# A recommendation tower on one core: the perceptron over pairs of tiles in place of single tiles

## The chip, the core and the metric

The kernel runs on one core of a Trainium2 chip. The metric is the device time of one execution in microseconds (us). Each engine runs its own instruction stream: TensorE (PE; its weight loads are listed apart as PEld), VectorE (DVE), ScalarE (ACT), GpSimd (POOL) and SyncE (SP). They meet only through semaphores and DMA.

## The reference

For 2048 samples, 32 embedding rows of 16 numbers are looked up, all 496 dot products of two of them are taken, and a perceptron of three layers (512, 256, 1) runs over these and 16 dense features. All is in float32.

```
e = jnp.stack([tbl_0[ids[:, 0]], ..., tbl_31[ids[:, 31]]], axis=1)     # [2048, 32, 16]
z = jnp.sum(e[:, row, :] * e[:, col, :], axis=2)                       # 496 pairs row < col of the 32 fields
h = jnp.concatenate([z, dense_ctx], axis=1)                            # [2048, 512]
h = jnp.maximum(h @ W_top1 + b_top1, 0.0)                              # 512 x 512
h = jnp.maximum(h @ W_top2 + b_top2, 0.0)                              # 512 x 256
y = h @ W_top3                                                         # 256 x 1
```

## The kernel before, in words

The samples are worked in 16 tiles of 128 (the partitions). Of the 32 fields, 17 have small tables (1000 or 1250 rows); these are kept on chip and looked up by TensorE with one-hot matrices in six "rounds" (`look_up`, L640 and L645), from which VectorE picks the row with a maximum (`pick`, L470). The other 15 fields are gathered from HBM by GpSimd, one indirect DMA for each field and tile (L367), in three groups of 7, 5 and 3 fields, written straight into `emb`, which has room for all tiles.

What sets the order on GpSimd: after every fifth gather (`RUN`) it waits until that gather has landed (L373), except in the last tile, 15, where the 15 gathers follow each other without this. From tile 2 on it also waits, ahead of each group, until VectorE has multiplied the same group two tiles earlier (L358).

VectorE multiplies the pairs (L480, L489, L498, L508) into `prod`, a group as soon as its fields have landed, and itself sums the last 112 pairs (`sum_pairs`, L517). TensorE sums and turns the other 384, in three chunks of 128: `sum_chunk` (L663) is 16 accumulating transposes, `turn` (L670) one for the chunk that VectorE summed. The result stands in PSUM with features on the partitions; ScalarE copies it to `zT` (`copy_z`, L882).

The perceptron of the program before takes one tile at a time, 128 samples as columns: `layer1(t, place, n)` for n = 0 to 3 (L683, 4 matmuls each of 128x128 weights by 128 columns, float32), `relu1` on ScalarE (L888), `layer2(t)` (L692, 8 matmuls), `relu2` (L893), `layer3(t)` (L699, 2 matmuls with a single weight column), `copy_y` (L899). A float32 matmul of this kind leaves two records in the trace (a transpose and a bf16 matmul leave one), so that one `layer1` chunk is 8 records and `layer2` is 16.

All engines step through "windows", one for each tile t, in an order written out by hand: in window t TensorE finishes chunk 2 and the turn of tile t-1, runs layers 2 and 3 of tile t-2, layer 1 of tile t-1, the look-ups of tile t+1 and the first round or two of t+2, and chunks 0 and 1 of tile t. Windows 0 and 1 are straight code, 2 to 13 a loop over pairs of windows, 14 straight again. The end (from L763 on TensorE, L968 on ScalarE) treats tile 15 with orders of its own: `add_chunks` (L780) runs layer 1 chunk by chunk as its inputs come, then layer 2 (L803) and layer 3 (L811). On ScalarE `relu1(14, 2)` and `relu1(14, 3)` stand ahead of `copy_end` (L981) and of the copies of the second group of tile 15 (`copy_group`, L875 and L877), on which VectorE's last products wait. The result is stored in two DMAs, the second of tile 15 alone (L335).

## Time and profile before

| | |
|---|---|
| median of 3 runs | 390.46 us (387.18, 390.46, 392.57) |
| span of the profiled execution | 386.4 us |
| time of the profiled execution | not listed apart; the nearest run is 387.18, 0.8 us above the span |
| TensorE, weight loads | 299.7 us busy (78%), 267.2 us (69%) |
| VectorE | 248.2 us (64%) |
| GpSimd | 228.5 us (59%) |
| ScalarE | 145.3 us (38%) |
| mean granted TensorE clock | 0.925 |

The span is that from the first to the last instruction on the core; what a run takes beyond it lies around it. A share of busy time says how much work an engine has, not whether anything waits for it. A gather counts as GpSimd's work only while the instruction runs, not while its data are under way.

### The profile page before, as it was taken

What the parts mean: (1) busy time and instruction counts of PE and PEld (TensorE: products, weight loads), DVE (VectorE), ACT (ScalarE), POOL (GpSimd) and SP (SyncE); (2) the same over time, 40 slices, a digit from 0 to 9 for tenths busy, and PEclk for the clock granted to TensorE, in tenths of its full rate; (3) what the DMA queues carried; (4) which work ended last, traced back from release to release, by engine and by line L of the source; (5) the groups of instructions that cost most, each with busy time, mean ns of one, the idle gap of its engine ahead of it and who ended that gap; (6) DMA issues with size and microseconds to landing.
All of it is one profiled execution on the core that took longest, in us unless ns stands there. A gap on an engine that the chain in (4) does not pass through costs nothing.

```text
span 386.4 us, 7087 instructions
## 1 busy us (share of the span) xinstructions
PE 299.7 (78%) x2572; PEld 267.2 (69%) x2572; DVE 248.2 (64%) x326; ACT 145.3 (38%) x311; POOL 228.5 (59%) x250
## 2 busy tenths in 40 slices
PE   1767799886987967988676887877699786978477
PEld 1356689785887856877665886766598675867366
DVE  7699758675666666493756739464683955557541
ACT  3883543443162525244332424424243441113012
POOL 6456655566566656656665666566556656666700
PEclk9889779998999999989999998999969899899859
DMA  6670020202020202102020110202002000000000
GB/s 141 205 242 7 8 64 8 64 8 65 7 63 5 65 5 49 21 6 63 6 64 5 40 29 6 64 6 65 6 9 60 5 7 5 8 6 8 6 2 3
DMA packets 19036, 14.51 MB, mean 38 GB/s; under 512 B 9727, under 2 KB 16461, under 8 KB 19022
## 3 DMA queue, kind: packets, MB, share of 16 engines
q1 hardware_dynamic: 10284, 11.69, 9.5%
q0 software_dynamic: 7680, 1.98, 5.9%
q10 hardware_dynamic: 1058, 0.66, 0.6%
q8 instruction: 8, 0.13, 0.1%
q14 instruction: 6, 0.05, 0.0%
HBM read 14.24 MB, written 0.08 MB: 37 GB/s over the span
## 4 chain that ended last, share of the span: by engine, by line
issue 33%; POOL 28%; DMA 15%; PE 9%; DVE 6%; another core or an unknown queue 4%; ACT 3%; DVEq 1%; ACTq 0%; POOLq 0%
POOL emb L367 28%; DMA emb<-tbl,idx 15%; DVE emb L470 2%; PE bank L683 2%; DVE prod L489 2%; PE bank L663 2%; PE bank L692 1%; PE bank L645 1%; PE bank L780 1%; DVE prod L498 1%; ACT h1T L888 1%; ACT distance L844 1%; ACT onehot L854 1%; DMA idx<-ids 1%
## 5 line engine op out<-in xcount | busy, mean ns | idle before, releaser
L367 POOL DMA_INDIRECT emb<-tbl,idx x240 | 227.3, 947 | 138.4 <-DMA emb<-tbl,idx 73.4
L489 DVE TENSOR_TENSOR prod<-emb,bank 128x1904 f32<-128x1904 f32 (+5 forms) x51 | 94.5, 1854 | 88.3 <-DMA emb<-tbl,idx 88.3
L663 PE MATMUL bank<-ident,prod 128*128 128x128 f32 x768 | 102.8, 287 | 14.0 <-issue 8.6
L663 PEld LDWEIGHTS bank<-ident,prod 128*128 128x128 f32 x768 | 94.4, 197 | 15.9 <-issue 9.9
L683 PE MATMUL bank<-zT,w_sb 128*128 128x128 f32 x480 | 70.6, 295 | 13.6 <-ACT zT L882 12.9
L645 PE MATMUL bank<-parts,onehot 125*128 125x160 bf16 (+1 forms) x816 | 77.0, 244 | 1.4 <-issue 1.3
L683 PEld LDWEIGHTS bank<-zT,w_sb 128*128 128x128 f32 x480 | 63.6, 207 | 16.7 <-issue 14.9
L645 PEld LDWEIGHTS bank<-parts,onehot 125*128 125x128 bf16 x816 | 66.2, 106 | 12.3 <-issue 4.6
L470 DVE TENSOR_REDUCE emb<-bank 128x480 f32 (+5 forms) x96 | 52.7, 584 | 17.2 <-PE bank L645 8.8
L640 PE MATMUL bank<-far_ten,named_ten 100*128 100x480 bf16 (+1 forms) x64 | 24.8, 388 | 33.1 <-issue 24.5
L888 ACT ACTIVATE h1T<-bank,b_sb 128x128 f32<-128x128 f32 x60 | 21.5, 363 | 65.9 <-PE bank L683 26.5
L875 ACT COPY bank<-emb 128x112 f32 (+3 forms) x32 | 7.8, 243 | 100.0 <-issue 81.2
L480 DVE TENSOR_TENSOR prod<-bank,emb 128x2176 f32<-128x2176 f32 x16 | 38.7, 2419 | 7.2 <-ACT bank L868 6.4
L517 DVE TENSOR_REDUCE z_last<-prod 128x22 f32<-128x352 f32 (+3 forms) x32 | 34.8, 1087 | 2.2
L854 ACT ACTIVATE onehot<-distance,one 125x1152 bf16<-125x1152 bf16 (+1 forms) x30 | 35.8, 1195 | 0.0
L844 ACT ACTIVATE distance<-gids,minus_row 125x1152 bf16<-125x1152 f16 (+1 forms) x30 | 34.4, 1193 | 0.2
L640 PEld LDWEIGHTS bank<-far_ten,named_ten 100*128 (+1 forms) x64 | 6.9, 108 | 39.1 <-issue 32.0
L692 PE MATMUL bank<-h1T,w_sb 128*128 128x128 f32 x240 | 31.9, 288 | 1.0 <-issue 0.8
L692 PEld LDWEIGHTS bank<-h1T,w_sb 128*128 128x128 f32 x240 | 29.7, 201 | 1.9 <-issue 1.5
L498 DVE TENSOR_TENSOR prod<-bank,emb 128x336 f32<-128x336 f32 (+1 forms) x32 | 13.2, 411 | 8.7 <-ACT emb L877 7.7
L882 ACT COPY zT<-bank 128x512 f32<-128x512 f32 x15 | 8.8, 585 | 25.7 <-remote 22.8
L640 PE MATMUL bank<-far_eight,named_eight 70*128 70x512 bf16 (+1 forms) x32 | 11.3, 354 | 8.2 <-DVE emb L470 5.1
(71 smaller groups left out, 126.5 us busy)
## 6 DMA issues: line engine op xcount, KB each, us to landing
gids<-small_ids_f SPq DMA_DIRECT2D x16, 544.0 KB
emb<-tbl,idx POOLq DMA_INDIRECT x240
w_sb<-w SPq DMA_DIRECT2D x1, 1024.0 KB
w_sb<-w SPq DMA_DIRECT2D x1, 512.0 KB
tab<-tbl SPq DMA_DIRECT2D x7, 56.0 KB
tab<-tbl SPq DMA_DIRECT2D x5, 70.0 KB
tab<-tbl ACTq DMA_DIRECT2D x5, 70.0 KB
z_last<-dense SPq DMA_DIRECT2D x16, 8.0 KB
```

Of the source, the lines that this page charges most:

```text
L367: nc.gpsimd.indirect_dma_start(emb[:, t, at:at + D], None, tables[f], bass.IndirectOffsetOnAxis(ap=idx[:, t, f:f + 1], axis=0)).then_inc(d ...
L470: nc.vector.tensor_reduce(emb_at(t, SMALL_PLACE + first, n).rearrange("p a x -> p (a x)"), bank[:, from_bank, 0:width_of(r)].rearrange("p ...
L480: nc.vector.tensor_tensor(prod[:, 0:PAIR_AT[1] * D].rearrange("p (k x) -> p k x", k=SHIFTS), strided(bank[:, E_BANK, 0:S * D], [[0, SHIFTS ...
L489: return nc.vector.tensor_tensor(prod[:, at * D:(at + n * a) * D].rearrange("p (j i d) -> p j i d", j=n, d=D), strided(emb_at(t, PLACES[g] ...
L517: nc.vector.tensor_reduce(z_last[:, place, first - SUM_AT:end - SUM_AT], prod[:, first * D:end * D].rearrange("p (a d) -> p a d", d=D), AX ...
L640: nc.tensor.matmul(bank[:, to_bank, 0:n * w], named[0:rows, bass.ts(t, P)], far[0:rows, field * w:(field + n) * w], start=True, stop=False)
L645: mm = nc.tensor.matmul(look, onehot[:, place, i, :], parts[:, k, CAND_AT[i] * D:CAND_AT[i + 1] * D], start=False, stop=(i == first + n - ...
L663: mm = nc.tensor.matmul(bank[:, Z_BANK + place, c * P:(c + 1) * P], v[:, d, :], ident[:], start=(d == 0), stop=(d == D - 1), is_transpose= ...
L683: mm = nc.tensor.matmul(bank[:, H1_BANK + n % 2, 0:P], w1_sb[:, c, n * P:(n + 1) * P], zT[:, place, c, :], start=(c == 0), stop=(c == CHUN ...
L692: mm = nc.tensor.matmul(bank[:, H2_BANK, m * P:(m + 1) * P], w2_sb[:, c, m * P:(m + 1) * P], h1T[:, c, :], start=(c == 0), stop=(c == H1 / ...
L844: nc.scalar.activation(distance[:, first * P:(first + n) * P].rearrange("p (f j n) -> p f j n", f=n, n=SUB), gids[0:ROWS, place, :].rearra ...
L854: nc.scalar.activation(onehot[:, place, first:first + n, :].rearrange("p f b -> p (f b)"), distance[:, first * P:(first + n) * P], ACT.Rel ...
```

## The change

Layers 1 to 3 now take "units". Units 0 to 6 are the tile pairs (0,1) to (12,13), with 256 columns a matmul; tiles 14 and 15 are units of one tile each, as before with 128 columns. `zT`, `h1T` and `h2T` hold two tiles side by side; the two results of a pair go to columns 256 to 511 of PSUM bank 4. In an even window t (2, 4, ...) TensorE runs chunks 0, 1 and 2 of layer 1 of the pair (t-2, t-1); in the odd window behind it chunk 3, both chunks of layer 2 and layer 3. Windows 0 and 1 hold no perceptron work any more. The weights, look-ups, sums, gathers, products and the treatment of tile 15 are the same. On GpSimd nothing is changed, and on VectorE only the semaphore counts at the end.

```diff
         z_last = sb("z_last", [P, 2, (CHUNKS - TURN_SUMS) * P])
-        zT = sb("zT", [P, 2, CHUNKS, P])
-        h1T = sb("h1T", [P, H1 // P, P])
-        h2T = sb("h2T", [P, H2 // P, P])
+        zT = sb("zT", [P, CHUNKS, 2, P])
+        h1T = sb("h1T", [P, H1 // P, 2 * P])
+        h2T = sb("h2T", [P, H2 // P, 2 * P])
         y = sb("y", [1, B])
         w1_sb = sb("w1_sb", [P, CHUNKS, H1])
         w2_sb = sb("w2_sb", [P, H1 // P, H2])
...
+
+        PAIR_Y_BANK = 4
 
         END_H1_BANK, END_H2_BANK = (3, 4, 6, 7), (5, 0)
...
+
+        PAIRS = TILES // 2 - 1
+        LAST_UNIT = PAIRS + 1
+
         def steps_done(t, step):
...
                 pe.wait_ge(dense_loaded[place], loads * 16)
                 turn(place, 3)
 
-            def layer1(t, place, n):
+            def z_of(c, half):
+
+                return zT[:, c, :, :].rearrange("p h b -> p (h b)") if half is None else zT[:, c, half, :]
+
+            def layer1(unit, n, tiles, half=None):
+                cols = P if half is not None else 2 * P
                 if n == 0:
-                    pe.wait_ge(z_copied, t + 1)
-                pe.wait_ge(h1_done, 4 * t + n + 1)
+                    pe.wait_ge(z_copied, tiles)
+                pe.wait_ge(h1_done, 4 * unit + n + 1)
+                if n == 1:
+                    pe.wait_ge(y_copied, unit + 1)
                 for c in range(CHUNKS):
-                    mm = nc.tensor.matmul(bank[:, H1_BANK + n % 2, 0:P], w1_sb[:, c, n * P:(n + 1) * P],
-                                          zT[:, place, c, :], start=(c == 0), stop=(c == CHUNKS - 1))
+                    mm = nc.tensor.matmul(bank[:, H1_BANK + n % 2, 0:cols], w1_sb[:, c, n * P:(n + 1) * P],
+                                          z_of(c, half), start=(c == 0), stop=(c == CHUNKS - 1))
                 mm.then_inc(h1_ready, 1)
 
-            def layer2(t):
-                pe.wait_ge(y_copied, t + 1)
-                pe.wait_ge(h1_done, 4 * t + 4 + 2)
-                for m in range(H2 // P):
-                    for c in range(H1 // P):
-                        mm = nc.tensor.matmul(bank[:, H2_BANK, m * P:(m + 1) * P], w2_sb[:, c, m * P:(m + 1) * P],
-                                              h1T[:, c, :], start=(c == 0), stop=(c == H1 // P - 1))
+            def layer2(unit, m, cols=2 * P, together=False):
+                if m == 0:
+                    pe.wait_ge(y_copied, unit + 1)
+                    pe.wait_ge(h1_done, 4 * unit + 4 + 2)
+                elif not together:
+                    pe.wait_ge(h2_done, 2 * unit + 1)
+                for c in range(H1 // P):
+                    mm = nc.tensor.matmul(bank[:, H2_BANK, m * cols:(m + 1) * cols], w2_sb[:, c, m * P:(m + 1) * P],
+                                          h1T[:, c, 0:cols], start=(c == 0), stop=(c == H1 // P - 1))
                 mm.then_inc(h2_ready, 1)
 
-            def layer3(t):
-                pe.wait_ge(h2_done, 2 * t + 2)
+            def layer3(unit, y_bank=PAIR_Y_BANK, cols=2 * P):
+                pe.wait_ge(h2_done, 2 * unit + 2)
                 for c in range(H2 // P):
-                    mm = nc.tensor.matmul(bank[0:1, H2_BANK, Y_COL:Y_COL + P], w3_sb[:, c:c + 1],
-                                          h2T[:, c, :], start=(c == 0), stop=(c == H2 // P - 1))
+                    mm = nc.tensor.matmul(bank[0:1, y_bank, Y_COL:Y_COL + cols], w3_sb[:, c:c + 1],
+                                          h2T[:, c, 0:cols], start=(c == 0), stop=(c == H2 // P - 1))
                 mm.then_inc(y_ready, 1)
 
-            def window(t, place, loads, before=2, look=True, ahead=True):
-
-                if before > 0:
-                    sum_chunk(t - 1, 1 - place, 2, GROUP1_STEP)
-                    turn_sums(t - 1, 1 - place, loads)
-                if before > 1:
-                    layer2(t - 2)
-                if before > 0:
-                    layer1(t - 1, 1 - place, 0)
-                if before > 1:
-                    layer3(t - 2)
-                if look:
-                    look_up_rounds(t + 1, 1 - place, (2, 3))
-                sum_chunk(t, place, 0, SMALL_STEP)
-                if before > 0:
-                    layer1(t - 1, 1 - place, 1)
-                else:
-
-                    pe.wait_ge(masks_made, 2 * n_masks)
-                    turn_masks(1)
-                if look:
-                    look_up_rounds(t + 1, 1 - place, (4, 5))
-                if before == 0:
-                    pe.wait_ge(named_made, 3)
-                    turn_masks(2)
-                sum_chunk(t, place, 1, CIRCLE0_STEP)
-                if before > 0:
-                    layer1(t - 1, 1 - place, 2)
-                else:
-                    pe.wait_ge(named_made, 6)
-                    turn_masks(3)
+            def first_window():
+
+                look_up_rounds(1, 1, (2, 3))
+                sum_chunk(0, 0, 0, SMALL_STEP)
+                pe.wait_ge(masks_made, 2 * n_masks)
+                turn_masks(1)
+                look_up_rounds(1, 1, (4, 5))
+                pe.wait_ge(named_made, 3)
+                turn_masks(2)
+                sum_chunk(0, 0, 1, CIRCLE0_STEP)
+                pe.wait_ge(named_made, 6)
+                turn_masks(3)
+                look_up_rounds(2, 0, (0,))
+                look_up_rounds(2, 0, (1,))
+
+            def even_window(t, unit, ahead=True):
+
+                sum_chunk(t - 1, 1, 2, GROUP1_STEP)
+                turn_sums(t - 1, 1, unit + 1)
+                look_up_rounds(t + 1, 1, (2, 3))
+                layer1(unit, 0, 2 * unit + 2)
+                sum_chunk(t, 0, 0, SMALL_STEP)
+                layer1(unit, 1, 2 * unit + 2)
+                look_up_rounds(t + 1, 1, (4, 5))
+                sum_chunk(t, 0, 1, CIRCLE0_STEP)
+                layer1(unit, 2, 2 * unit + 2)
                 if ahead:
-                    look_up_rounds(t + 2, place, (0,))
-                if before > 0:
-                    layer1(t - 1, 1 - place, 3)
-                if ahead:
-                    look_up_rounds(t + 2, place, (1,))
+                    look_up_rounds(t + 2, 0, (0,))
+                    look_up_rounds(t + 2, 0, (1,))
+
+            def odd_window(t, unit, loads, after_pair=True):
+
+                if after_pair:
+                    layer1(unit, 3, 2 * unit + 2)
+                sum_chunk(t - 1, 0, 2, GROUP1_STEP)
+                turn_sums(t - 1, 0, loads)
+                look_up_rounds(t + 1, 0, (2, 3))
+                sum_chunk(t, 1, 0, SMALL_STEP)
+                if after_pair:
+                    layer2(unit, 0)
+                look_up_rounds(t + 1, 0, (4, 5))
+                sum_chunk(t, 1, 1, CIRCLE0_STEP)
+                if after_pair:
+                    layer2(unit, 1)
+                look_up_rounds(t + 2, 1, (0,))
+                if after_pair:
+                    layer3(unit)
+                look_up_rounds(t + 2, 1, (1,))
 
             pe.wait_ge(masks_made, n_masks)
             pe.wait_ge(ident_bf_ready, 1)
...
+            odd_window(1, 0, 1, after_pair=False)
             with pe.Fori(0, (TILES - 4) // 2) as j:
-                window(2 * j + 2, 0, j + 1)
-                window(2 * j + 3, 1, j + 2)
-            window(TILES - 2, 0, TILES // 2 - 1, ahead=False)
+                even_window(2 * j + 2, j)
+                odd_window(2 * j + 3, j, j + 2)
+            even_window(TILES - 2, PAIRS - 1, ahead=False)
+            layer1(PAIRS - 1, 3, TILES - 2)
 
             t = LAST_TILE
             sum_chunk(t - 1, 0, 2, GROUP1_STEP)
-            layer2(t - 2)
-            layer3(t - 2)
+            layer2(PAIRS - 1, 0)
+            layer2(PAIRS - 1, 1, together=True)
+            layer3(PAIRS - 1)
             turn_sums(t - 1, 0, TILES // 2)
-            layer1(t - 1, 0, 0)
-            layer1(t - 1, 0, 1)
+            layer1(PAIRS, 0, t, half=0)
+            layer1(PAIRS, 1, t, half=0)
             sum_chunk(t, 1, 0, SMALL_STEP)
-            layer1(t - 1, 0, 2)
-            layer1(t - 1, 0, 3)
+            layer1(PAIRS, 2, t, half=0)
+            layer1(PAIRS, 3, t, half=0)
             sum_chunk(t, 1, 1, CIRCLE0_STEP)
...
 
-            def relu1(t, n):
-                act.wait_ge(h1_ready, 4 * t + n + 1)
-                nc.scalar.activation(h1T[:, n, :], bank[:, H1_BANK + n % 2, 0:P], ACT.Relu,
+            def relu1(unit, n, cols=2 * P):
+                act.wait_ge(h1_ready, 4 * unit + n + 1)
+                nc.scalar.activation(h1T[:, n, 0:cols], bank[:, H1_BANK + n % 2, 0:cols], ACT.Relu,
                                      bias=b1_sb[:, n:n + 1]).then_inc(h1_done, 1)
 
-            def relu2(t, m):
-                act.wait_ge(h2_ready, t + 1)
-                nc.scalar.activation(h2T[:, m, :], bank[:, H2_BANK, m * P:(m + 1) * P], ACT.Relu,
+            def relu2(unit, m, cols=2 * P, together=False):
+                act.wait_ge(h2_ready, 2 * unit + (2 if together else m + 1))
+                nc.scalar.activation(h2T[:, m, 0:cols], bank[:, H2_BANK, m * cols:(m + 1) * cols], ACT.Relu,
                                      bias=b2_sb[:, m:m + 1]).then_inc(h2_done, 1)
 
-            def copy_y(t):
-                act.wait_ge(y_ready, t + 1)
+            def copy_pair_y(unit):
+                act.wait_ge(y_ready, unit + 1)
                 act.nop(nofuse=True)
...
+                copy_group(0, 1, GROUP1_STEP)
...
-                    onehots(t + 2, place, 1)
-                if before > 0:
-                    relu1(t - 1, 1)
-                else:
-                    copy_named(2)
+                    onehots(t + 2, 0, 1)
+                relu1(unit, 1)
                 copy_group(t, 1, GROUP1_STEP)
-                if before == 0:
-                    copy_named(3)
-                if look:
-                    wrap(t + 1)
-                if before > 0:
-                    relu1(t - 1, 2)
-                    relu1(t - 1, 3)
-                if before > 1:
-                    copy_y(t - 2)
-                if look:
-                    copy_small(t + 1)
+                wrap(t + 1)
+                relu1(unit, 2)
+                if not ahead:
+                    relu1(unit, 3)
+                copy_small(t + 1)
+
+            def odd_window(t, unit, loads, after_pair=True):
+
+                distances(t + 2, 1, 0, loads)
+                distances(t + 2, 1, 1, loads)
+                if after_pair:
+                    relu1(unit, 3)
+                copy_z(t - 1, 0)
+                onehots(t + 2, 1, 0)
+                copy_group(t, 0, GROUP0_STEP)
+                onehots(t + 2, 1, 1)
+                if after_pair:
+                    relu2(unit, 0)
+                copy_group(t, 1, GROUP1_STEP)
+                wrap(t + 1)
+                if after_pair:
+                    relu2(unit, 1)
+                    copy_pair_y(unit)
+                copy_small(t + 1)
 
             act.dma_start(idx[:, 0, :], ids[:, 0, :]).then_inc(first_ids_loaded, 16)
```

In the loop on TensorE one turn handles two tiles. Of before, from the first window of a turn to the third chunk of layer 1 (L683 is layer 1, L692 layer 2, L699 layer 3, L663 a chunk of sums, L640 and L645 the look-ups):

```order
70 L683 MATMUL bank<-zT,w_sb 128x128 x4
72 L699 MATMUL bank<-h2T,w_sb 1x128 x2
76 L645 MATMUL bank<-parts,onehot 128x160 x6
79 L645 MATMUL bank<-parts,onehot 128x160 x6
81 L663 MATMUL bank<-ident,prod 128x128 x16
83 L683 MATMUL bank<-zT,w_sb 128x128 x4
```

Of the changed program, the same stretch (L696 is layer 1):

```order
65 L651 MATMUL bank<-parts,onehot 128x160 x6
68 L651 MATMUL bank<-parts,onehot 128x160 x6
71 L696 MATMUL bank<-zT,w_sb 128x256 x4
73 L669 MATMUL bank<-ident,prod 128x128 x16
75 L696 MATMUL bank<-zT,w_sb 128x256 x4
```

The instructions are as many for a pair as they were for a tile, with twice the columns, and the first chunk of layer 1 now stands behind the look-ups.

TensorE after window 14, before (from the last layer 1 of tile 13 to the second half of layer 1 of tile 14):

```order
162 L683 MATMUL bank<-zT,w_sb 128x128 x8
163 L663 MATMUL bank<-ident,prod 128x128 x16
164 L692 MATMUL bank<-h1T,w_sb 128x128 x8
165 L699 MATMUL bank<-h2T,w_sb 1x128 x2
166 L670 MATMUL bank<-ident,z_last 128x128
167 L683 MATMUL bank<-zT,w_sb 128x128 x8
168 L663 MATMUL bank<-ident,prod 128x128 x16
169 L683 MATMUL bank<-zT,w_sb 128x128 x8
170 L663 MATMUL bank<-ident,prod 128x128 x16
```

and now:

```order
145 L696 MATMUL bank<-zT,w_sb 128x256 x8
146 L669 MATMUL bank<-ident,prod 128x128 x16
147 L707 MATMUL bank<-h1T,w_sb 128x256 x8
148 L714 MATMUL bank<-h2T,w_sb 1x256 x2
149 L676 MATMUL bank<-ident,z_last 128x128
150 L696 MATMUL bank<-zT,w_sb 128x128 x8
151 L669 MATMUL bank<-ident,prod 128x128 x16
152 L696 MATMUL bank<-zT,w_sb 128x128 x8
153 L669 MATMUL bank<-ident,prod 128x128 x16
```

The order is the same; the three steps that belonged to tile 13 now belong to the pair (12,13) and have 256 columns.

ScalarE in the same stretch, before and, behind the dots, now:

```order
157 L882 COPY zT<-bank 128x512
158 L888 ACTIVATE h1T<-bank,b_sb 128x128 x2
159 L875 COPY bank<-emb 128x112
160 L877 COPY emb<-emb 128x48
161 L888 ACTIVATE h1T<-bank,b_sb 128x128 x2
162 L981 COPY zT<-bank 128x256
...
147 L911 COPY zT<-bank 128x4x128
148 L917 ACTIVATE h1T<-bank,b_sb 128x128 x2
149 L904 COPY bank<-emb 128x112
150 L906 COPY emb<-emb 128x48
151 L917 ACTIVATE h1T<-bank,b_sb 128x128 x2
152 L1032 COPY zT<-bank 128x2x128
```

Nothing moved here: the copies of the first group of tile 15 still stand behind the first two rectifications of tile 14, and `copy_end` behind the other two.

## Rows read from the trace of the kernel before

**Rows 1.** The page, part 1: busy us, share of the span and instructions of each engine.

```profile
PE 299.7 (78%) x2572; PEld 267.2 (69%) x2572; DVE 248.2 (64%) x326; ACT 145.3 (38%) x311; POOL 228.5 (59%) x250
```

**Rows 2.** Waits of the whole span: engine line, waited for, us in total, times, longest.

```profile
DVE prod L489 <- DMA emb<-tbl,idx: 88.3, 25, 5.3
POOL emb L367 <- DMA emb<-tbl,idx: 73.4, 42, 4.8
POOL emb L367 <- DVE prod L498: 4.9, 3, 1.7
```

**Rows 3.** Groups by line, GpSimd's gathers: count, busy us, mean ns, idle before, releaser.

```profile
L367 POOL DMA_INDIRECT emb<-tbl,idx x240 | 227.3, 947 | 138.4 <-DMA emb<-tbl,idx 73.4
```

**Rows 4.** Timeline, GpSimd: start, us, instruction, idle before and releaser; first, later, last gathers.

```profile
3.01 1.11 POOL L367 DMA_INDIRECT emb<-tbl,idx  x1 [1.00 <-DMA idx<-ids]
...
356.77 0.95 POOL L367 DMA_INDIRECT emb<-tbl,idx  x1 [0.30 <-issue]
...
366.78 0.95 POOL L367 DMA_INDIRECT emb<-tbl,idx  x1 [0.30 <-issue]
```

**Rows 5.** Timeline, VectorE, a tile of the steady part: the two large group products.

```profile
201.39 2.14 DVE L489 TENSOR_TENSOR prod<-emb,bank 128x1904 f32<-128x1904 f32 x1 [4.63 <-DMA emb<-tbl,idx]
...
208.52 2.15 DVE L489 TENSOR_TENSOR prod<-emb,bank 128x1920 f32<-128x1920 f32 x1 [3.59 <-DMA emb<-tbl,idx]
```

**Rows 6.** Busy us of each engine in four steady windows, then clock and DMA.

```profile
163.00:254.00 91.00, 71.75 (x637) 65.36 (x637) 56.92 (x64) 33.45 (x72) 56.76 (x60) 0.94 0.13 30
```

**Rows 7.** Timeline, 193 to 220: TensorE, GpSimd and ScalarE in and behind one window.

```profile
193.44 0.33 PE L670 MATMUL bank<-ident,z_last 128*128 128x128 f32 x1
193.60 2.00 PE L692 MATMUL bank<-h1T,w_sb 128*128 128x128 f32 x16
...
196.97 0.59 ACT L882 COPY zT<-bank 128x512 f32<-128x512 f32 x1 [2.69 <-remote]
197.32 0.95 POOL L367 DMA_INDIRECT emb<-tbl,idx  x1 [1.61 <-DMA emb<-tbl,idx]
...
198.77 0.60 PE L699 MATMUL bank<-h2T,w_sb 128*1 128x128 f32 x4
```

**Rows 8.** Timeline of the end, 344 to 385.

```profile
344.12 1.87 PEld L683 LDWEIGHTS bank<-zT,w_sb 128*128 128x128 f32 x16
344.23 1.95 PE L683 MATMUL bank<-zT,w_sb 128*128 128x128 f32 x16
...
347.61 2.07 PE L663 MATMUL bank<-ident,prod 128*128 128x128 f32 x16 [1.43 <-issue]
...
357.65 1.95 PE L683 MATMUL bank<-zT,w_sb 128*128 128x128 f32 x16
...
359.17 2.14 DVE L489 TENSOR_TENSOR prod<-emb,bank 128x1904 f32<-128x1904 f32 x1 [4.04 <-DMA emb<-tbl,idx]
...
362.35 1.17 PE L663 MATMUL bank<-ident,prod 128*128 128x128 f32 x8 [2.75 <-DVE prod L498]
...
370.55 0.63 ACT L888 ACTIVATE h1T<-bank,b_sb 128x128 f32<-128x128 f32 x2 [8.79 <-remote]
...
371.32 3.71 PE L692 MATMUL bank<-h1T,w_sb 128*128 128x128 f32 x16 [0.19 <-ACT h1T L888]
...
375.06 1.17 DVE L517 TENSOR_REDUCE z_last<-prod 128x61 f32<-128x976 f32 x1
...
380.07 0.27 PE L670 MATMUL bank<-ident,z_last 128*128 128x128 f32 x1
```

**Rows 9.** Stretch behind the break in TensorE's chunk: columns as in Rows 6.

```profile
364.50:371.30 6.80, 2.75 (x7) 1.16 (x8) 0.95 (x1) 0.75 (x3) 2.62 (x3) 0.51 0.07 5
```

**Rows 10.** Groups by line, ScalarE: rectification and copies for the perceptron.

```profile
L888 ACT ACTIVATE h1T<-bank,b_sb 128x128 f32<-128x128 f32 x60 | 21.5, 363 | 65.9 <-PE bank L683 26.5
...
L882 ACT COPY zT<-bank 128x512 f32<-128x512 f32 x15 | 8.8, 585 | 25.7 <-remote 22.8
...
L899 ACT COPY y<-bank 1x128 f32 (+1 forms) x16 | 3.9, 241 | 2.5 <-PE bank L811 1.4 <-PE bank L699 1.1
```

116 lines of the change are left out of this document (62 added, 54 removed).

## The prediction

> **What bounds the kernel now.** I first read the shares of busy time [rows 1]. TensorE has the most work, 78% of the span, and the change shortens just that work. A share does not say who waits, so the list of waits comes next [rows 2]: VectorE spends 88.3 us waiting for gathered rows to land, and GpSimd's own waits are for its own gathers. Then I add up GpSimd's queue: 240 gathers are busy for 227.3 us with 138.4 us of idle time between them [rows 3], together 365.7 us. The first gather starts at 3.01 and the last ends at 366.78 + 0.95 = 367.7 [rows 4]. With the 2 us ahead of the first, the account closes: nothing else is in it. One tile is 15 gathers of 0.947, twelve pauses of 0.30 and three waits for a landing of some 1.6, that is 22.7 us; four tiles make 91 us, and a stretch of 91 us in the steady part holds 60 gathers [rows 6].
>
> Does another engine hold GpSimd? The only such wait of note is put down to VectorE three times, 4.9 us in all [rows 2], 1.6 each, as long as a landing takes anyway. GpSimd waits for the products of two tiles earlier, while VectorE multiplies a group of the same tile as soon as it has landed: its large product starts at 359.17, 1.45 us behind the end of the gather at 356.77 + 0.95 [rows 4, 8]. So there is more than one tile, 22 us, in hand. In the steady part VectorE sits idle for 4.63 and 3.59 us ahead of the two large products of a tile [rows 5]: TensorE's look-ups and ScalarE's copies, which stand ahead of these, may come some 3 us later without any effect.
>
> What is left is the end. By that 1.45 us the last gather lands at about 369.2, and the span ends at 386.4, 17.2 us later. There TensorE's second chunk of tile 15 starts at 362.35 and breaks off after 8 of 16 transposes [rows 8]. The next 6.8 us hold 7 records at a granted clock of 0.51, that is 1.2 GHz, behind a thin stretch [rows 9]; the same chunk elsewhere takes 2.07 us. ScalarE waits 8.79 us, until 370.55, for layer 1 of tile 14, whose matmuls ended at 359.60 by the records [rows 8]. The profile names no releaser. A smaller case of the kind is in the steady part: the turn at 193.44 is over at 193.8, but ScalarE copies its result only at 196.97, after 2.69 us of idling, just ahead of GpSimd's restart at 197.32 [rows 7]. My reading is that signals from TensorE, and at worst its issue, come late while gathers are under way, and that the last tile, whose 15 gathers have no wait between them, shows this at its longest. That is read from two coincidences, not shown.
>
> **The change, part by part.**
>
> Steady part, TensorE. The width costs as follows. Layer 3 has weights of one column, so nothing but the 128 moving columns can set its pace: 4 records in 0.60 us [rows 7], the last of them 0.27 long as a lone one is [rows 8], so (0.60 - 0.27) / 3 = 0.11 us each. At 256 columns I take 0.22 us a record. The bounds are 0.117, the pace of the weight loads (1.87 us for 16 [rows 8]), which is no more than now, and 0.244, twice the 1.95 / 16 of layer 1. A pair of tiles has now 96 records of layers 1 and 2 at 0.122 = 11.7 us and two times 0.60; after, 48 at 0.22 = 10.6 and 1.04: 1.3 us less for a pair, 9 us for seven pairs. All of it lies beside GpSimd's queue. It is costed at nothing: the gathers cover it, and without that cover it would be the rival below.
>
> The Trainium skill, "TensorE: Matmul & The Clock Gate", section "Back-to-back issue gap", gives for streams of weight load and matmul about 81 ns at 128 columns and 131 ns at 512, which makes added columns far cheaper than the row of layer 3 does. As an estimate from that page, 256 columns cost 1.2 times what 128 do, and a pair would save 4.7 us rather than 1.1 in layers 1 and 2. No row here has a wide float32 matmul, so the trace doesn't decide between them yet.
>
> Steady part, waits. Layer 1's first chunk moves behind the look-ups, which favours VectorE. In odd windows ScalarE's copy for the next tile's small products stands behind `copy_pair_y`, and so behind layer 3, which stands behind a look-up round that waits for VectorE's fifth pick. Before, `relu1(t-1, 3)` stood at the same place behind the same round. A half-us more is inside the 3 us above. Nothing for this, with bounds 0 and 0, as GpSimd has a tile in hand. ScalarE does half as many rectifications; a wide one costs 0.363 + 128 x (0.585 - 0.363) / 384 = 0.44 us [rows 10], not twice. It is 38% busy: nothing. The first windows lose layer 1 of tile 0; GpSimd doesn't wait there either: nothing. GpSimd, SyncE's DMAs and the gathers stay: nothing.
>
> The end is the one place with a price. Three steps of tile 13 now are steps of the pair (12,13). The last half of layer 1 at 344.23, 16 records, grows from 1.95 to 15 x 0.22 + 0.38 = 3.7 us, by 1.7; TensorE idled 1.43 behind it ahead of 347.61 [rows 8], so 0.3 are left. Layer 2 grows by 1.7, its two rectifications by 0.15, layer 3 by 0.4, the copy of y (0.241 now [rows 10]) by 0.05. Together 2.6 us. The chain behind these (turn, copy of z, layer 1 of tile 14 around chunk 0 of tile 15) keeps its length, and its end goes from 357.65 + 1.95 = 359.6 to 362.2. The next chunk couldn't start before 362.35, since it waits for VectorE, and TensorE was idle for 2.75 us ahead of it [rows 8]. So the 2.6 us just fit. By the upper bound of 0.244, with wide ScalarE steps at double price, they are 4.0 and 1.3 us stick out; by the lower nothing does. From the second chunk of tile 15 on, the instructions are the same.
>
> **Sum:** 386.4 + 0 = 386.4 us of span, bounds 0 and +1.3. The fastest run shown is 0.8 above that span, and the median, 390.46, is 4.1 above. I carry the difference over to the median: **390.5 us**.
>
> **The rivals.**
>
> (a) The break at the end goes away or shrinks. The chunk at 362.35 would end at 364.4 and layer 2 of tile 14, which now starts at 371.32, at about 364.5, at full clock in 2.0 instead of 3.71 us [rows 7, 8]. The turn at 380.07 comes 8.75 behind that start; less 1.7 it would be at 371.6. VectorE allows that: the last landing at 369.2 leaves 2.4 us for its last products and its sum of 1.17 [rows 8]. That is 8.5 us less: 382.0. For it: TensorE sends half the instructions in the layers, if their number is what clogs. Against it: GpSimd's 15 gathers are the same, and TensorE is as densely loaded up to 362. Chance 0.20, half of it a partial gain of about 4 us.
>
> (b) Slower: the late signal moves one step up. ScalarE's first two rectifications of tile 14 now come 2.6 us later, at about 358 to 359, in the time from which signals weren't seen before 370.55, and the copies for VectorE's next product stand behind them. It decides whether the signal of chunk 1 of that layer is given before the late stretch begins, which lies somewhere before 359.6. If not, VectorE's product that TensorE's second chunk waits for, over at 362.3 now [rows 8], moves to 371.7, the second chunk runs from 371.7 to 373.7 or, at half clock, 375.4, instead of ending at 371.1: 2.6 to 4.3 more, plus a rectification: +4, 394.5 us. Chance 0.12.
>
> (c) TensorE falls to 1.2 GHz ahead of the last chunk. Rows show what it costs: 3.71 against 2.00 us for 16 records [rows 7, 8], 1.7 more, of which 0.15 fit: 392.0. Less TensorE work leaves longer gaps, and the one fall in these rows came after a thin stretch [rows 9]. Against it, the last tiles get denser, not thinner. Chance 0.06. The Trainium skill, same page, section "HAM oscillation — how this bites in real kernels", says that gaps between bursts of matmuls bring the half clock back; the fall in the last tile agrees, and by that rule a kernel with shorter bursts would lose on every window, which here the gathers would hide but for the end.
>
> (d) TensorE, the busiest engine, does set the pace: 9 us less, 381.4. Against it stands the closed account of the gathers. By the page's column price it would be some 33 us less, 358. Chance 0.04; as much goes to the change not working as it says, a wait of a window on the wrong count, with a time that I can't work out.
>
> **How the numbers follow.** The main case, an unchanged end, has 0.54, and is 388 to 393, as wide as the runs of before scatter and with the 1.3 above. (a) reaches from 382 to 388, (b) and (c) from 392 to 395. 383.5 to 394 leaves out about 0.2: the full case of (a), (d), and the upper part of (b). A measurement of this kernel tells about 2% from no change, that is 382.7 and 398.3. Faster by more: half of (a) and (d), 0.12. Slower by more: 0.03, from (b) with more than I work out and the unknown. Within 2%: 0.85.
>
> **What would show it.** Right: the last gather ends near 367.7 again, VectorE still waits some 88 us for landings, TensorE's busy time falls by about 9 us to 290, a layer 1 chunk pair of 16 wide records takes 3.7 us (2.4 would speak for the page), layer 1 of tile 14 ends near 362, and ScalarE again waits some 8 us, until about 370. Wrong: gathers that end earlier or later, a ScalarE wait ahead of the first two rectifications of tile 14 (b), or a second chunk of tile 15 in one piece of 2 us (a).

## The result

| | median | runs |
|---|---|---|
| kernel before | 392.53 us (387.18 to 397.34) | 20 |
| changed kernel | 393.73 us (388.75 to 395.51) | 20 |

Ratio of the undisturbed runs, changed to before: **1.0171, 95% interval 1.0115 to 1.0227**. The medians are only 0.3% apart, because the ratio leaves out the runs more than 1.5% above a kernel's fastest, 7 of the 20 of the kernel before and 4 of the changed one. So how much slower the changed kernel is here, 0.3 or 1.7%, depends on how the scatter is treated. I had forecast 390.5 us and no change. The time lies within my range, but by the ratio the kernel got slower by more than its interval, and the first trace already shows that my picture of the kernel did not hold.

Profiled execution after: 392.63 us, span 390.8 (386.4 before). The page's shares, for [rows 1]:

```profile
PE 294.4 (75%) x2208; PEld 248.2 (64%) x2208; DVE 247.3 (63%) x326; ACT 136.3 (35%) x262; POOL 228.2 (58%) x250
```

The waits after, for [rows 2], and the group of the gathers, for [rows 3]:

```profile
DVE prod L495 <- DMA emb<-tbl,idx: 125.8, 30, 6.3
POOL emb L373 <- DMA emb<-tbl,idx: 86.9, 42, 6.1
```

```profile
L373 POOL DMA_INDIRECT emb<-tbl,idx x240 | 227.0, 946 | 151.7 <-DMA emb<-tbl,idx 86.9
```

TensorE does 5.3 us less, as many instructions as planned are gone, and that is hidden. But GpSimd, which the change doesn't touch, idles 13.3 us longer between its gathers, all of it for landings. Its queue in one window of the steady part after, with what SyncE issues meanwhile:

```profile
222.03 0.94 POOL L373 DMA_INDIRECT emb<-tbl,idx  x1 [0.30 <-issue]
222.67 1.65 DVE L523 TENSOR_REDUCE z_last<-prod 128x90 f32<-128x1440 f32 x1
...
224.96 0.27 PE L676 MATMUL bank<-ident,z_last 128*128 128x128 f32 x1
225.27 0.33 SPq L307 DMA_DIRECT2D z_last<-dense  x1
225.64 0.43 SPq L303 DMA_DIRECT2D gids<-small_ids_f  x1
225.77 0.94 POOL L373 DMA_INDIRECT emb<-tbl,idx  x1 [0.30 <-issue]
230.40 0.94 POOL L373 DMA_INDIRECT emb<-tbl,idx  x1 [3.68 <-DMA emb<-tbl,idx]
```

The turn at 224.96 ends the tile's sums; SyncE waits for it (`summed`), loads the dense features and then the ids of a later tile, 544 KB. Here that load starts 0.13 us ahead of the fifth gather, for whose landing GpSimd then waits 3.68 us instead of the 1.6 of [rows 7]. Such waits of 2.6 to 3.7 us stand in 8 of the 12 steady tiles. The end after, for [rows 4, 8]:

```profile
356.56 3.62 PE L696 MATMUL bank<-zT,w_sb 128*128 128x256 f32 x16
...
362.76 3.69 PE L707 MATMUL bank<-h1T,w_sb 128*128 128x256 f32 x16 [0.15 <-ACT h1T L917]
...
373.07 1.95 PE L696 MATMUL bank<-zT,w_sb 128*128 128x128 f32 x16
...
374.74 0.69 ACT L917 ACTIVATE h1T<-bank,b_sb 128x128 f32<-128x128 f32 x2
...
375.43 2.07 PE L669 MATMUL bank<-ident,prod 128*128 128x128 f32 x16 [0.41 <-DVE prod L504]
...
379.76 0.94 POOL L373 DMA_INDIRECT emb<-tbl,idx  x1 [0.30 <-issue]
```

The last gather ends at 379.76 + 0.94 = 380.7, 13.0 us later than [rows 4]. The second chunk of tile 15 (375.43) runs in one piece and ScalarE has no wait of 8.8 us as in [rows 8], so only 10.1 us lie behind the last gather, not 18.7. 13.0 less 8.6 is 4.4, the difference of the spans. No wait of this trace is put down to "remote" (the profile's word where it can name no releaser), while before has some 60 us of them. So two things changed that the edit doesn't name, and the first question was whether it made them.

There is a hint on record that it did not. Wherever a run's span is listed, the run takes 1.8 to 2.0 us more than its span. So the trace of before, with a span of 386.4, belongs to an execution of about 388.3 us, and none of the 20 runs of that kernel in the table above has this time (the nearest are 387.62 and 390.0). It was not one of the runs that the changed kernel is compared with.

### The profile page after: what moved, and what is told of

Read it like the earlier page. It is cut to its first block, busy times and chain, and to the rows that moved or that the text cites. A ratio compares the mean times of both kernels' runs of the same rounds, so it can differ in the third digit from the quotient of the medians.

```text
span 390.8 us, 6259 instructions
## 1 busy us (share of the span) xinstructions
PE 294.4 (75%) x2208; PEld 248.2 (64%) x2208; DVE 247.3 (63%) x326; ACT 136.3 (35%) x262; POOL 228.2 (58%) x250
## 4 chain that ended last, share of the span: by engine, by line
POOL 46%; DMA 24%; issue 24%; PE 3%; DVE 2%; POOLq 0%; DVEq 0%; ACT 0%
POOL emb L373 46%; DMA emb<-tbl,idx 24%; PE bank L809 1%; PE bank L669 1%; DVE prod L495 1%; DVE emb L476 1%; DVE prod L504 1%; DMA idx<-ids 1%; PE bank L832 0%; PE bank L707 0%; POOLq L116 0%; PE bank L714 0%; PE bank L840 0%; DVE h2T L616 0%; DVEq L476 0%
## 5 line engine op out<-in xcount | busy, mean ns | idle before, releaser
L669 PE MATMUL bank<-ident,prod 128*128 128x128 f32 x768 | 105.7, 296 | 0.8 <-DVE prod L504 0.4
L669 PEld LDWEIGHTS bank<-ident,prod 128*128 128x128 f32 x768 | 100.5, 199 | 2.3 <-DVE prod L495 0.8
L651 PE MATMUL bank<-parts,onehot 125*128 125x160 bf16 (+1 forms) x816 | 75.8, 243 | 0.0
L646 PE MATMUL bank<-far_ten,named_ten 100*128 100x480 bf16 (+1 forms) x64 | 23.5, 367 | 60.8 <-DVE emb L476 54.9
L696 PE MATMUL bank<-zT,w_sb 128*128 128x256 f32 (+1 forms) x256 | 61.4, 388 | 0.7 <-ACT zT L911 0.7
L696 PEld LDWEIGHTS bank<-zT,w_sb 128*128 128x128 f32 x256 | 47.2, 202 | 6.3 <-ACT zT L911 0.9
L707 PE MATMUL bank<-h1T,w_sb 128*128 128x256 f32 (+1 forms) x128 | 28.9, 372 | 0.2 <-ACT h1T L917 0.2
L707 PEld LDWEIGHTS bank<-h1T,w_sb 128*128 128x128 f32 x128 | 22.9, 198 | 2.6 <-issue 0.3
L917 ACT ACTIVATE h1T<-bank,b_sb 128x256 f32<-128x256 f32 (+1 forms) x32 | 14.3, 450 | 27.7 <-PE bank L696 27.7
L646 PEld LDWEIGHTS bank<-far_eight,named_eight 70*128 (+1 forms) x32 | 3.3, 102 | 26.0 <-issue 24.9
```

What stands on the lines that cost most here:

```text
L646: nc.tensor.matmul(bank[:, to_bank, 0:n * w], named[0:rows, bass.ts(t, P)], far[0:rows, field * w:(field + n) * w], start=True, stop=False)
L651: mm = nc.tensor.matmul(look, onehot[:, place, i, :], parts[:, k, CAND_AT[i] * D:CAND_AT[i + 1] * D], start=False, stop=(i == first + n - ...
L669: mm = nc.tensor.matmul(bank[:, Z_BANK + place, c * P:(c + 1) * P], v[:, d, :], ident[:], start=(d == 0), stop=(d == D - 1), is_transpose= ...
L696: mm = nc.tensor.matmul(bank[:, H1_BANK + n % 2, 0:cols], w1_sb[:, c, n * P:(n + 1) * P], z_of(c, half), start=(c == 0), stop=(c == CHUNKS ...
L707: mm = nc.tensor.matmul(bank[:, H2_BANK, m * cols:(m + 1) * cols], w2_sb[:, c, m * P:(m + 1) * P], h1T[:, c, 0:cols], start=(c == 0), stop ...
```

## Experiments

The sets are given in the order in which they ran; the kernels of a set ran on one chip, with runs of the kernel before among them. Which chip the traces above come from is not on record.

### First set: is it the load of ids?

The kernel before, for a second trace:

> The kernel before, once more, for a second trace of it. What has to be seen is whether two features of its first trace are fixed or chance: (1) the turn's signal (L670 to the load of the dense features, L301) comes 1.7 to 3.5 us late and lands on the moment at which the fifth gather of the tile has landed, so that the load of the ids (L297, 544 KB) starts in GpSimd's pause; (2) TensorE's second chunk of tile 15 breaks off for 6.8 us. Theory A (both belong to the order of the program before): both are there again, last gather ends at 367 to 369, span 386 to 387. Theory B (chance of one execution): the lags or the break are absent or elsewhere, and the gathers end some 10 us later or the end is some 8 us shorter.

Measured: 389.31 us, span 387.5. The group of its gathers:

```profile
L367 POOL DMA_INDIRECT emb<-tbl,idx x240 | 227.2, 947 | 148.3 <-DMA emb<-tbl,idx 85.1 <-issue 59.1 <-DVE prod L498 3.1
```

Ten us more idle time than in [rows 3], nine waits of 2.6 to 3.3 us, the last gather ending at 377.5, the span 10.0 us behind it, no break in the chunk. The unchanged kernel shows both features of the changed one: neither belongs to the edit.

That also says which traces to compare. Against this one, the changed kernel's last gather ends 3.2 us later (380.7 and 377.5) and its span 3.3 us later, not 13.0 and 4.4. The 3.3 us are there by the last gather of tile 3, changed and before:

```profile
99.74 0.94 POOL L373 DMA_INDIRECT emb<-tbl,idx  x1 [0.30 <-issue]
```

```profile
96.44 0.94 POOL L367 DMA_INDIRECT emb<-tbl,idx  x1 [0.30 <-issue]
```

In the changed kernel the long waits begin in tile 2 (3.1 us, then 3.4 in tile 3), in the kernel before in tile 4. From there on its single waits are longer, but three tiles have none, and up to the last gather the two kernels lose about the same. This is one trace of each.

The changed kernel whose load of ids waits until the fifth gather has landed (a "gate"):

```diff
                     sp.wait_ge(distance_made, stretches_done(t - 1, len(STRETCHES) - 1))
+                    sp.wait_ge(landed[0][t % 2], 16 * ((t - 2) // 2 * GROUPS[0] + RUN))
                     load_gids(t + 1)
```

> The changed kernel with one wait more on SyncE: the load of the ids of tile t+1 waits until the fifth gather of tile t-2 has landed. Theory A (in the changed kernel this load starts while the fourth or fifth gather of the tile is under way, and delays the landing on which GpSimd waits, by 1.3 to 2 us in 8 of 12 tiles, 13 us in all): all waits of GpSimd after tile 2 are 1.6 to 1.8 us, the last gather ends at about 368 to 369 in place of 380.7, and the time falls by some 12 us, to about 381. Rival (the gathers are slower for another reason, such as TensorE's wide reads): GpSimd's waits of 3 us stay, and the time stays within 1% of the changed kernel.

Measured: **379.10 us** (378.58 to 379.71), ratio 0.9845 (0.9694 to 0.9996). The kernel before had a median of 391.45 in this set, so by the medians it is 0.968; the ratio rests on 3 of its 13 runs. SyncE and GpSimd around the same place, apart:

```profile
218.13 0.32 SPq L303 DMA_DIRECT2D gids<-small_ids_f  x1
```

```profile
218.32 0.94 POOL L374 DMA_INDIRECT emb<-tbl,idx  x1 [1.56 <-DMA emb<-tbl,idx]
...
365.30 0.95 POOL L374 DMA_INDIRECT emb<-tbl,idx  x1 [0.31 <-issue]
```

The load starts in GpSimd's pause, 0.2 us ahead of its restart; from tile 2 to 13 no wait is over 1.7 us (one of 3.1 stands ahead of the last tile), and the last gather ends at 366.25 instead of 380.7. One edited line that moves nothing but a load takes 14 us off the gathers.

Two kernels that should have moved the load in the kernel before. In the first a marker on GpSimd behind its fourth gather starts it:

```diff
+                    sp.wait_ge(fourth, t - 1)
                     load_gids(t + 1)
...
+                        if g == 0 and i == 3:
+                            pool.nop(nofuse=True).then_inc(fourth, 1)
```

On SyncE this load moves ahead of that of the dense features, too.

> The kernel before with nothing changed in its layers, but with the load of the ids of tile t+1 issued just after GpSimd has issued the fourth gather of tile t-2 (a marker on GpSimd's queue, and on SyncE this load stands ahead of that of the dense features). Theory A (the collision of this load with the fifth gather is the whole price): GpSimd's wait ahead of the sixth gather becomes 3 us in most of 12 tiles, the gathers end 15 to 20 us later, time 3.5 to 5% above before. Rival (the load is harmless, and the width or order of the layers slows the gathers): no change beyond the markers, under 1%.

Measured: 379.68 us, ratio 0.9879 (0.9701 to 1.0057), by the medians 0.970. It missed its purpose: the load started only once the 15th gather had landed, so it fell into that pause. It became another gate: last gather at 366.5, two waits of 2.3 and 2.7 us and no others. So in this set the kernel before and the changed one, each with a gate, take 379.7 and 379.1 us: nothing is left of a difference once the load is out of the way, though the two gates are not the same. In the second, look-ups go ahead of layer 2, so that the turn's neighbours move:

```diff
+                if look:
+                    look_up_rounds(t + 1, 1 - place, (2, 3))
                 if before > 1:
                     layer2(t - 2)
...
-                if look:
-                    look_up_rounds(t + 1, 1 - place, (2, 3))
```

> The kernel before, single tiles and 128 columns, with one move on TensorE: in every window the look-up rounds 2 and 3 of tile t+1 stand directly behind the turn, and layer 2 of tile t-2 behind them. Theory A (the order, not the width, made the turn's signal prompt, since TensorE then waits instead of running on): the lag of the turn's signal falls from 2-3 us to about 0, the ids are loaded 2 to 3 us earlier, in several tiles on top of the fourth or fifth gather, and the gathers end 5 to 15 us later; time 1 to 4% above before unless the end gets shorter. Rival (the width matters): lags and gathers as before, within 1%.

Measured: 388.2 us, ratio 1.0067 (0.9982 to 1.0153), by the medians 0.992, six waits of 2.2 to 3.5 us and a last gather at 371.5. Same mechanism, another mix; it doesn't tell the theories apart.

### Second set: gate and pairs apart

> The kernel before with the wait of e2 on SyncE: the load of the ids of tile t+1 not before the fifth gather of tile t-2 has landed. The second trace of before (e1) had 9 waits of 2.6 to 3.3 us on GpSimd. Theory A (these come from the load, in both kernels): no wait above 1.8 us after tile 2, last gather ends at 366 to 368, time 378 to 381, as e2 and e3; against e6 in the same call it shows what the pairs are worth by themselves: within 0.5%. Rival (the pairs themselves gain once the collisions are gone): e6 is over 1% faster than this.

> The kernel of e2 once more, in one call with e5: 379 us, as before. Theory A: within 0.5% of e5, since GpSimd's gathers set the pace in both and the end of both is some 10 us behind the last gather. Rival: over 1% faster than e5, by the 9 us less of TensorE work.

Measured: before with the gate 390.18, ratio 1.0023 (1.0001 to 1.0044); changed with the gate, the very kernel that took 379.1, **389.83**, ratio 1.0018 (0.9992 to 1.0044); the kernel before had a median of 389.19. The expected gain was missing in both. Both end their last gather at 369.8 with no long wait from tile 2 on, and then take 19 us. The end of the second of them:

```profile
364.82 0.27 PE L670 MATMUL bank<-ident,prod 128*128 128x128 f32 x1
...
368.27 0.37 PE L670 MATMUL bank<-ident,prod 128*128 128x128 f32 x1 [1.82 <-issue]
...
372.50 2.18 PE L670 MATMUL bank<-ident,prod 128*128 128x128 f32 x9 [0.22 <-issue]
372.67 0.62 ACT L918 ACTIVATE h1T<-bank,b_sb 128x128 f32<-128x128 f32 x2 [8.60 <-remote]
```

The broken chunk and ScalarE's long wait of [rows 8] are back, with 256 columns as with 128. So they go with the executions, not with the kernel: on this chip all show waits put down to "remote", in the first set none did. I call the two kinds of execution late and prompt, for a reason that the third set shows. Between themselves the two differ by 0.1%: pairs by themselves are worth nothing here, as forecast.

To have the price of the load alone, it starts in the kernel before when the third gather has landed, which is just ahead of the fifth; and, the other way, it brings 128 of its 2176 columns from tile 4 on (the look-ups of those tiles then use old ids, so the results of the small tables are left out). In the first, the load again stands ahead of that of the dense features on SyncE:

```diff
+                    sp.wait_ge(third[t % 2], 16 * ((t - 2) // 2 + 1))
                     load_gids(t + 1)
```

```diff
+                n = S * P if t < 4 else P
```

> The cost by itself, which e3 missed because its marker came late: the kernel before, single tiles, with the load of the ids of tile t+1 started by the landing of the third gather of tile t-2 (a semaphore of its own), which is some 0.2 us ahead of the start of the fifth. Theory A (the price depends on where the load starts, and just ahead of the fifth gather it is dearest): GpSimd's wait ahead of the sixth gather is 3.2 to 3.7 us in nearly all of 12 tiles, the last gather ends at 383 to 388, the time is 394 to 400, slower than both kernels. Rival (collisions cost some 1.2 us wherever they fall): the time stays at 391 to 393.

> The kernel before with its order and waits, but from tile 4 on the load of the ids brings only 128 of 2176 columns (32 KB in place of 544 KB; so the look-ups of those tiles use old ids). Theory A (it is the transfer of 544 KB that holds up the gather's landing): all waits of GpSimd 1.5 to 1.8 us from tile 3 on, time 378 to 382 without any gate. Rival (the issue of a DMA by SyncE, or TensorE's signals at that moment, hold it up, not the bytes): the waits of 2.8 us stay, 388 to 392.

Measured: 413.59, ratio **1.0629 (1.0592 to 1.0667)**, and 388.46, ratio 0.9981 (0.9958 to 1.0004). A window of the first:

```profile
208.69 0.94 POOL L372 DMA_INDIRECT emb<-tbl,idx  x1 [0.30 <-issue]
209.89 0.32 SPq L298 DMA_DIRECT2D gids<-small_ids_f  x1
209.94 0.94 POOL L372 DMA_INDIRECT emb<-tbl,idx  x1 [0.30 <-issue]
212.20 0.33 SPq L302 DMA_DIRECT2D z_last<-dense  x1
214.61 0.94 POOL L372 DMA_INDIRECT emb<-tbl,idx  x1 [3.73 <-DMA emb<-tbl,idx]
```

The load 0.05 us ahead of the fifth gather, and 3.73 us of waiting; so in 11 tiles (3.2 to 3.7), and the last gather ends at 393.1, where that of the small load, on the same chip, ends at 367.7. Of these 25 us the 11 collisions are 20, at 1.8 each; the rest are longer waits in tiles 0 and 1 (4.6 and 3.4 us) and two of 2.2. The time is above the 394 to 400 expected for two reasons: the last gather was forecast at 383 to 388, and I had added the short end, where this chip has the long one. The small load, forecast at 378 to 382, tells little, as there was nothing to avoid here: from tile 2 on all waits ahead of the sixth gather are 1.5 to 1.7 us, but so they are in this chip's trace of the unchanged kernel (next set).

### Third set: the same chip again, and pauses in the last tile

> The kernel before once more, to have its trace beside the next three. Theory C (two kinds of executions, the same for all kernels of one chip): either every kernel of this set shows waits of ScalarE put down to nothing that the profile knows and a second chunk of tile 15 that breaks up, then this one has gaps of 1.6 us, a last gather that ends near 367.7 and 18.7 us behind it, 389 to 391 us; or none does, then it has gaps of 2.6 to 3.3 us in most tiles, a last gather that ends at 374 to 378 and 10 us behind it, 387 to 390 us. Theory D (each kernel brings its own kind with it): this one and the next may differ.

> The changed kernel once more. Theory C: of the same kind as the trace beside it. In the kind with prompt signals: gaps of 3.2 to 3.7 us ahead of the sixth gather in 8 or 9 tiles, last gather ending at 379 to 381, 10 us behind it, 392 to 394 us, 1.0 to 1.5% above the kernel before. In the kind with late signals: the load of ids falls into GpSimd's pause, gaps of 1.6 us, last gather near 369.8, 19 us behind it, 389.5 to 391 us, within 0.3% of the kernel before. Theory D: prompt signals and 392 to 394 us whatever the trace beside it shows.

> The changed kernel whose load of ids waits for the landing of the fifth gather. Theory C: with prompt signals all gaps at 1.6 us, last gather at 366 to 367, 11 us behind it, 379 us, 3% below the kernel before; with late signals last gather at 369.8, 19 us behind it, 390 us, no different. The rival, that the 379 us seen once had another cause than the gaps, expects about the time of the run before it.

In the last of the set GpSimd waits in the last tile too:

```diff
+                        if t == LAST_TILE and place == RUN - 1:
+                            pool.wait_ge(done, 16 * (t // 2 * n + i + 1))
+                        if t == LAST_TILE and place == 2 * RUN - 1:
+                            pool.wait_ge(done, 16 * (i + 1))
```

> The same with GpSimd waiting in the last tile too for the landing of its fifth and tenth gather, as it does in every other tile. If late signals come from gathers that are issued without a pause, the two pauses cost GpSimd 2 x 1.3 us, and with late signals the second chunk of tile 15 runs in one piece and ScalarE's wait of 8.6 us goes: 10 to 12 us behind the last gather instead of 19, 384 to 386 us in all. With prompt signals the two pauses only cost: 381 to 382 us against 379. If the late signals have nothing to do with the pauses: 392 us with late signals.

Measured: 387.97; **388.67**, ratio 0.9978 (0.9955 to 1.0001); 389.68, ratio 1.0023 (1.0 to 1.0047); and **384.15** (381.82 to 386.67), ratio 0.9873 (0.9784 to 0.9963). The changed kernel's loss is gone without any edit, in a trace that has no long wait from tile 2 on. A turn in that trace (second of the set):

```profile
193.77 0.27 PE L676 MATMUL bank<-ident,z_last 128*128 128x128 f32 x1
194.84 0.94 POOL L373 DMA_INDIRECT emb<-tbl,idx  x1 [0.30 <-issue]
197.06 0.33 SPq L307 DMA_DIRECT2D z_last<-dense  x1
197.06 0.59 ACT L911 COPY zT<-bank 128x512 f32<-128x512 f32 x1 [2.56 <-remote]
197.43 0.43 SPq L303 DMA_DIRECT2D gids<-small_ids_f  x1
197.49 0.94 POOL L373 DMA_INDIRECT emb<-tbl,idx  x1 [1.71 <-DMA emb<-tbl,idx]
```

ScalarE and SyncE wait for the same signal of TensorE. The matmul ended at 194.04; both start at 197.06, 3.0 us later and 0.4 ahead of GpSimd's restart. In the trace of after above SyncE started 0.04 us behind the matmul. A late signal pushes the load into GpSimd's pause, where it is harmless: on such a chip a kernel whose load hangs on the turn has the gate for nothing. Since the profile models the ends of matmuls, it does not show whether the signal is late or the matmul itself.

With the two pauses the end of the last kernel:

```profile
364.10 0.62 ACT L922 ACTIVATE h1T<-bank,b_sb 128x128 f32<-128x128 f32 x2
364.79 2.07 PE L674 MATMUL bank<-ident,prod 128*128 128x128 f32 x16 [1.70 <-issue]
...
370.57 0.94 POOL L374 DMA_INDIRECT emb<-tbl,idx  x1 [0.30 <-issue]
```

The chunk runs whole and the long wait is gone. The last gather ends at 371.5, 3.9 us later than in the kernel without pauses, and the span at 381.6, 10.1 us behind it. The two differ by nothing but the pauses, 389.68 and 384.15 us: the long end comes from gathers issued without a pause.

### Fourth set: a third chip, and a surprise

> The changed kernel a third time, in more rounds, beside the kernel before (next). With prompt signals, as in the first trace of it: load of ids with or shortly ahead of the fifth gather in 8 or 9 tiles, gaps there of 3.2 to 3.7 us, last gather ending at 379 to 381, 392 to 394 us, and 1 to 1.5% above the kernel before. With late signals: gaps of 1.6 us, 388.5 to 390.5 us, within 0.3% of the kernel before, as in the run before this set.

> The kernel before on the same chip as the run above. With prompt signals 9 or so gaps of 2.6 to 3.3 us, last gather ending at 374 to 378, some 3 to 4 us ahead of that of the run above; with late signals 366.7 to 367.7, within 1 us of it.

> The changed kernel with the gated load of ids and the two pauses in the last tile. With late signals 384 us as before, ratio 0.987; with prompt signals the gate is worth 10 to 12 us and the pauses cost 2.6: 381 to 382 us, ratio 0.97 to 0.98. A version that is better than both kernels on both kinds of chip would be one by either.

> The kernel before with the two pauses in the last tile and nothing else. With late signals, if the pauses alone bring the short end: last gather near 370.3, 10 us behind it, 382 to 384 us, and neither the pairs nor the gate have a part in it. If the pairs have a part in it (fewer instructions of TensorE in the last tile): 386 us or more. With prompt signals: 1.3 to 2.6 us slower than the kernel before, 391 to 393 us.

| kernel | median | ratio |
|---|---|---|
| before | 414.95 (408.77 to 419.48) | |
| changed | 388.56 (386.41 to 389.61) | **0.9413** (0.9347 to 0.9479) |
| changed, gate and pauses | 384.56 | 0.9337 (0.9249 to 0.9426) |
| before, pauses | 403.35 | 0.9751 (0.9652 to 0.9850) |

By the medians the three are 0.936, 0.927 and 0.972. The changed kernel, with and without the edits, takes what I expected with late signals.

No theory had the kernel before at 415 us. Its gathers don't explain it: the last ends at 370.1, that of the changed kernel at 367.1. What GpSimd and VectorE do near the end, kernel before:

```profile
369.13 0.94 POOL L367 DMA_INDIRECT emb<-tbl,idx  x1 [0.30 <-issue]
...
386.38 1.65 DVE L517 TENSOR_REDUCE z_last<-prod 128x90 f32<-128x1440 f32 x1
```

and the changed kernel's same sum:

```profile
350.47 1.65 DVE L523 TENSOR_REDUCE z_last<-prod 128x90 f32<-128x1440 f32 x1
```

This is VectorE's last sum of tile 14, whose last gather starts at 349.06 and 346.04. It ends 39.0 us behind that in the kernel before and 6.1 in the changed one. In the former VectorE waits for no landings at all in the stretch from 212 to 303; the chain TensorE, ScalarE, VectorE has fallen behind GpSimd, from 15 us at tile 1 on, at (388.0 - 65.1) / 13 = 24.8 us a tile against the gathers' 23.0. TensorE isn't full meanwhile (71.7 of 91 us), nor slower: its granted clock is 0.94 there, as in [rows 6]. What holds it, in the kernel before:

```profile
230.04 0.37 ACT L888 ACTIVATE h1T<-bank,b_sb 128x128 f32<-128x128 f32 x1 [2.88 <-PE bank L683]
230.27 0.94 POOL L367 DMA_INDIRECT emb<-tbl,idx  x1 [1.69 <-DMA emb<-tbl,idx]
...
237.65 0.63 ACT L888 ACTIVATE h1T<-bank,b_sb 128x128 f32<-128x128 f32 x2 [4.67 <-remote]
237.88 0.94 POOL L367 DMA_INDIRECT emb<-tbl,idx  x1 [1.68 <-DMA emb<-tbl,idx]
...
245.21 0.59 ACT L882 COPY zT<-bank 128x512 f32<-128x512 f32 x1 [4.29 <-remote]
245.48 0.95 POOL L367 DMA_INDIRECT emb<-tbl,idx  x1 [1.65 <-DMA emb<-tbl,idx]
```

ScalarE moves on at 230.04, 237.65 and 245.21, each time 0.2 to 0.3 us ahead of GpSimd's restart. I read this as steps that have locked to the grid of GpSimd's pauses, three to a tile; a chain in which more than three such handovers follow one on another then needs more than a tile's time. The waits of ScalarE's first rectification show the difference, before and changed:

```profile
ACT h1T L888 <- remote: 70.0, 21, 6.9
ACT h1T L888 <- PE bank L683: 59.0, 26, 5.7
```

```profile
ACT h1T L917 <- PE bank L696: 23.2, 10, 5.4
...
ACT h1T L917 <- remote: 13.3, 3, 8.4
```

47 waits and 129 us became 13 and 36.5. The pairs halve the handovers of the perceptron, and here they are worth 26 us. That the number of handovers is the cause is read from these traces; no kernel varied the number alone. The expectation for the pauses alone (382 to 384) missed for the same reason: the chain is 31 us behind at tile 14 there. Nor are the 12 us by which that kernel came down shown to be the pauses' work. VectorE's sum of tile 14 is 8.4 us less behind than in the kernel before (30.6 against 39.0), and the pauses stand only in tile 15: most of the difference was there before them.

### Fifth set: a fourth chip, prompt signals

> The changed kernel once more, against the kernel before, wherever the chip puts the two. By the reading so far the changed kernel is 386 to 390 us with late signals, whatever the kernel before takes there (389 on one chip, 415 on another), and 392 to 394 us with prompt ones, where the kernel before takes 388 to 391 and so is 1% faster. If it is under 390 us with prompt signals, or if its gaps ahead of the sixth gather are 1.6 us there, the reading of the first measurement is wrong.

> The kernel before with the gated load of ids. With prompt signals: all gaps 1.6 us, last gather at 365 to 367, 10 us behind it, 377 to 380 us, as the changed kernel with the gate (379.1): then the pairs cost nothing by themselves there either. With late signals and 389 us for the kernel before: 389 to 390 again. With late signals and 415 us for the kernel before: 410 to 420, as the gate does nothing for TensorE's late signals.

Measured: kernel before 395.01 (391.95 to 397.74), changed 391.72 (390.94 to 392.88), ratio **0.9895 (0.9843 to 0.9948)**; before with the gate 382.24 (380.35 to 383.87), ratio **0.9676 (0.9619 to 0.9732)**. The two traces of this set, of the changed kernel and of before with the gate, have no "remote" waits. The changed kernel comes at the time expected, within 0.3 us of it, and its trace is like its first one, with eight waits of 2.9 to 3.5 us:

```profile
L373 POOL DMA_INDIRECT emb<-tbl,idx x240 | 226.6, 944 | 151.6 <-DMA emb<-tbl,idx 88.2 <-issue 59.1 <-DVE prod L504 3.2
...
231.21 0.94 POOL L373 DMA_INDIRECT emb<-tbl,idx  x1 [3.48 <-DMA emb<-tbl,idx]
```

But it is faster than the kernel before (0.992 by the medians), not slower as I expected. Since the gate takes 13 us off the kernel before, that one too must lose time to the load there; how many collisions it has is not known, as it has no trace in this set. So which of the two is ahead with prompt signals is not settled by the kind of execution: 1.7% slower and 1.1% faster were both measured. The gate gives 3% there for the kernel before, at 382.2 us some 2 above the 377 to 380 expected. For the changed kernel, 379.1 on the first chip stands against 391.7 to 393.7 without it in other sets, so some 3% too.

### The collision's price by its place

From the traces of all sets, tile 2 on, where the load of ids starts, counted from the start of the fifth gather of a tile, and how long GpSimd then waits:

| load starts | wait |
|---|---|
| 2.5 us ahead or earlier | 1.5 to 1.8 us, but two of 2.3 and 2.7 |
| 0.6 to 0.2 us ahead | 2.6 to 3.2 us |
| 0.2 ahead to 0.5 behind | 2.9 to 3.7 |
| 0.7 behind (one case) | 2.2 |
| 0.8 behind or later | 1.5 to 1.8, once 2.0 |

Two further waits, of 2.1 and 2.2 us, have no load near them. What made the few that fit no row is open.

Where VectorE keeps up, its sum ends 6.1 to 6.3 us behind the start of the 15th gather, and the fifth gather of the next tile starts at 7.5 to 7.7. In the prompt trace of the kernel before the turn is over 0.46 us behind the sum, from tile 4 on; in the changed one it is 0.5, 0.9 or 2.1, which fits the wide work of TensorE that stands ahead of it (no run varied this alone). The load of ids follows 0.4 behind. So the kernel before loads at some 7.0, 0.4 to 0.6 ahead of that gather; the changed one at 7.1, or at 7.5, the worst place, or at 8.7, which is free. But the 0.46 is not fixed either: with the gate, and the same order on TensorE, the kernel before has 0.5, 1.7 or 2.9 in its prompt trace, so without the gate some of its loads could fall 0.7 or 1.9 behind the gather, where they cost little or nothing. That may be why its times scatter so much with prompt signals (382 to 395 us in the first set); no trace shows it.

## Why the prediction was wrong

**The failed step** is "GpSimd, SyncE's DMAs and the gathers stay: nothing." The account of GpSimd's queue, 365.7 us, closed, and I took its 1.6 us waits as a fixed price. They are the price when the load of ids misses them. That load hangs on the turn, the turn on TensorE, and the change moves TensorE's work by tenths of a microsecond: no one waits longer for that, but the load lands on a gather or beside it. The waits it lands on are 2.6 to 3.7 us instead of 1.6. In [rows 7] the turn is over at 193.8 and everything behind it starts at 197; I read the lateness there as a smaller case of trouble at the end, and never asked what would start earlier were it gone. The answer was a 13 us longer queue, 367.7 to 380.7. Of these the second trace of the kernel before has 10 without the change, and 3 are left to it. None of my rivals had a longer queue: the slower one, (b), had its price at the end.

The account [rows 3, 4] was right for its own trace. The step from it, that other executions of the same kernel have the same queue, was an assumption that I did not state.

**How the end would go.** The main case, an unchanged end, and rival (a), which had the break gone for a saving of 8.5 us, were both argued from what TensorE sends. The end was 8.6 us shorter in the first trace after, the size of (a) nearly to the digit. That is luck. The cause wasn't the one of (a): the unchanged kernel has the short end in the first set, and the changed one has the long end in the second and third. What removes it where signals are late are two pauses of GpSimd. Nothing of (b) or (c) shows in that trace: ScalarE doesn't wait ahead of the first rectifications of tile 14 beyond 1.3 us, the granted clock from 372 us to the end is 1.00, and layer 2 of tile 14 takes 1.95 us.

**The reading of late signals** was right as a mechanism (signals of TensorE come late while gathers are under way, longest in the last tile without pauses), and its weight was wrong. I said VectorE had "some 3 us" to spare and left it at that. On one chip the kernel before falls behind its gathers, and the changed kernel is 6% faster; by the traces that is the lateness times the number of handovers. My rival (d), TensorE sets the pace, is nearest, but by busy time it gave 9 us, and TensorE is busy for no more than 71.7 of 91 us there.

**Terms that held.** That TensorE's smaller work would be hidden held: with the gate, changed and before take the same time, 389.83 and 390.18. The widened steps of tiles 12 and 13 do fit. Sixteen wide records take 3.62 and 3.69 us, 3.7 forecast; layer 3 of the pair at the end 1.02 (1.04), though the seven average 1.46; ScalarE's wide rectification has a median of 0.46 (0.44). The Trainium skill, "TensorE: Matmul & The Clock Gate", section "Back-to-back issue gap", gives 81 ns at 128 columns and 131 ns at 512, and my estimate from it was 2.4 us for 16 wide records. The traces don't agree: in float32 here 16 records take 1.95 us at 128 columns and 3.62 at 256.

**Two sizes that were off.** TensorE's busy time fell by 5.3 us to 294.4, where I had said 9 and 290; the 768 records of the sums read 105.7 us in this trace against 102.8 in that of before. And in the chances, half of (a) and (d) make 0.14 for faster by more, not 0.12.

**No single number was right to expect.** Against the same kernel before, the changed one measured 1.7% slower, 0.2% faster, 5.9% faster and 1.1% faster (by the medians 0.3% slower, 0.2, 6.4 and 0.8% faster), and its own medians of 388.6 to 393.7 are steadier than the 389 to 415 of the kernel before. What makes a chip's signals late or prompt, and why one late chip takes the kernel before to 415 and another leaves it at 389, stays open; no run varied it.

The best version depends on it too: changed with the gate, 379.1 with prompt signals and 389.8 with late ones; with gate and pauses 384.2 and 384.6 with late ones. With prompt signals that one wasn't run.

## What to carry to other kernels

A wait for a small transfer has no fixed price: look at which large transfer may start beside it and what starts that one, and tie the large one to a point behind the wait. If a signal in the trace comes late, ask both what waits for it and what it keeps from starting early. And take more than one trace of the kernel before, from more than one set of runs, before calling an account closed: one of 386 us and one of 387 us hid queues that differ by 10 us and ends that differ by 9.

## What the runs showed of the hardware

- A direct load of 544 KB, which takes 3.7 to 3.9 us from issue to landing (medians of the traces that list it), makes GpSimd's wait for the landing of a gather up to 2.1 us longer if it starts between 0.6 us ahead and 0.5 us behind the start of that gather, and no longer from 0.8 us behind on.
- In all six traces of two chips SyncE follows TensorE's turn 0.02 to 0.04 us behind the matmul's end; on two others, under the same gathers, mostly 0.6 to 3.3 us behind it, and in the kernel that had fallen behind up to 5, just ahead of the restart of GpSimd at its pause. There, in 15 gathers without a pause, ScalarE waits 8.4 to 8.8 us wherever the chain keeps up.
- On the latter, GpSimd's gathers themselves are not slower: 944 to 947 ns in the mean in all traces.
